# A one-row gate sum moved from TensorE matmuls to VectorE multiply-adds, in a four-layer conditional residual block

## The reference

```python
x = x + L0(x, lang)      # adapter 256 -> 64 -> 256 and a layer norm
x = x + L1(x, subj)      # one 256x256 matrix, chosen by subject
x = x + L2(x, type)      # five two-layer networks and a gate
x = x + L3(x, type)      # masked softmax pooling over the 512 rows

def L2(h, type_idx, ...):
    s0, s1, s2 = (relu(h @ share_wi[n]) @ share_wo[n] for n in range(3))      # 256 -> 1024 -> 256
    expert_out = out_a * wa + out_b * wb                                      # two experts, mixed
    gi = concatenate([expert_out[:, 0], s0[:, 0], s1[:, 0], s2[:, 0]])        # row 0 only, 4*256 numbers
    g = softmax(relu(gi @ gate_w1) @ gate_w2)                                 # gate_w1 is 1024x256, gate_w2 256x4
    return expert_out * g[0] + s0 * g[1] + s1 * g[2] + s2 * g[3]
```

## Time and profile before

| | |
|---|---|
| median of 3 runs | 563.62 us (563.46 to 563.65) |
| the profiled execution's own time | 563.65 us |
| its span, first to last instruction | 561.4 us |
| TensorE busy | 546.3 us, 97% of the span |
| VectorE, ScalarE, GpSimd busy | 316.3 us (56%), 262.7 us (47%), 257.8 us (46%) |
| mean granted clock of TensorE | 0.99 |
| chain that ended last | PE 91%, DVE 4%, the rest 1% or less each |

### The profile page before, as it was taken

The page is one execution under the profiler, slowest core; times in us unless marked ns, Lnnn a source line. Parts: engine busy times, 40 slices in busy tenths (PEclk is TensorE's granted clock), DMA queues, the critical chain, the costliest instruction groups (busy, mean ns, idle before and its releaser), DMA issues.

```text
span 561.4 us, 7437 instructions
## 1 busy us (share of the span) xinstructions
PE 546.3 (97%) x2724; PEld 452.3 (81%) x2727; DVE 316.3 (56%) x528; ACT 262.7 (47%) x481; POOL 257.8 (46%) x209
## 2 busy tenths in 40 slices
PE   5999999999999999999999999999999999999995
PEld 3578888888888788788888788888888878889984
DVE  3877323684366395566237478457326649522377
ACT  3345544443456562535246555334335647443343
POOL 1475355445244373444434447334524537744044
PEclk9899999999999999999899999999989999999999
DMA  5424424222224325024203422322222222420002
GB/s 155 142 100 145 122 76 150 76 75 76 75 76 123 93 77 165 27 73 129 83 20 118 144 97 76 112 76 76 75 75 77 76 75 88 138 76 0 2 1 76
DMA packets 44460, 49.34 MB, mean 88 GB/s; under 512 B 7300, under 2 KB 34184, under 8 KB 44424
## 3 DMA queue, kind: packets, MB, share of 16 engines
q1 hardware_dynamic: 43624, 47.81, 26.4%
q10 hardware_dynamic: 800, 1.05, 0.6%
HBM read 46.76 MB, written 2.10 MB: 87 GB/s over the span
## 4 chain that ended last, share of the span: by engine, by line
PE 91%; DVE 4%; POOL 1%; SPq 1%; issue 1%; DMA 1%; ACT 1%; DVEq 0%; POOLq 0%; ACTq 0%
PE ps_hid L707 13%; PE ps_hid L712 13%; PE ps_net L762 13%; PE ps_hid L708 13%; PE ps_net L763 13%; PE ps_net L767 12%; PE ps_side L561 2%; PE ps_side L424 1%; PE ps_side L429 1%; PE ps_side L425 1%; PE ps_net L736 1%; DMA beta<-in_L_cond_beta_dram 1%; PE ps_hid L546 1%; PE ps_side L625 1%; PE ps_side L631 1%
## 5 line engine op out<-in xcount | busy, mean ns | idle before, releaser
L1432 DVE SCALAR_TENSOR_TENSOR hid_lo<-ps_hid,hid_hi 128x512 fp32r<-128x512 f32 x160 | 110.2, 689 | 194.3 <-ACT hid_hi L937 194.0
L1514 POOL TENSOR_TENSOR wi_lo<-raw_wi,wi_hi 128x512 fp32r<-128x512 f32 x80 | 108.0, 1350 | 242.9 <-ACT wo_hi L918 142.6
L937 ACT ACTIVATE hid_hi<-ps_hid 128x512 fp32r<-128x512 f32 x160 | 95.5, 598 | 224.3 <-PE ps_hid L712 224.1
L707 PE MATMUL ps_hid<-x2T_hi,wi_lo 128*128 128x512 f32 (+1 forms) x338 | 127.8, 380 | 0.2 <-POOL wo_lo L1515 0.2
L708 PE MATMUL ps_hid<-x2T_hi,wi_hi 128*128 128x512 f32 (+1 forms) x338 | 127.0, 378 | 0.0
L762 PE MATMUL ps_net<-hid_hi,wo_hi 128*128 128x512 f32 x304 | 122.9, 404 | 0.0
L763 PE MATMUL ps_net<-hid_hi,wo_lo 128*128 128x512 f32 x304 | 120.0, 395 | 0.0
L1515 POOL TENSOR_TENSOR wo_lo<-raw_wo,wo_hi 128x512 fp32r<-128x512 f32 x80 | 106.5, 1331 | 0.0
L712 PE MATMUL ps_hid<-x2T_lo,wi_hi 128*128 128x512 f32 (+1 forms) x338 | 100.4, 378 | 1.1 <-DVE x2T_lo L1389 1.1
L767 PE MATMUL ps_net<-hid_lo,wo_hi 128*128 128x512 f32 x304 | 94.7, 393 | 0.0
L707 PEld LDWEIGHTS ps_hid<-x2T_hi,wi_lo 128*128 128x128 f32 x338 | 63.5, 188 | 12.5 <-POOL wo_lo L1515 0.4
(11 more groups left out here) (269 smaller groups left out, 608.4 us busy)
## 6 DMA issues: line engine op xcount, KB each, us to landing
raw_wi<-in_L_cond_share_wi_dram SPq DMA_DIRECT2D x23, 512.0 KB, 3.7
raw_wo<-in_L_cond_share_wo_dram SPq DMA_DIRECT2D x23, 512.0 KB, 4.7
raw_wi<-in_L_cond_expert_wi_dram SPq DMA_DIRECT2D x16, 512.0 KB, 3.6
raw_wo<-in_L_cond_expert_wo_dram SPq DMA_DIRECT2D x16, 512.0 KB, 4.6
x_rows<-in_x_dram SPq DMA_DIRECT2D x3, 512.0 KB, 6.1
out_dram<-out_rows SPq DMA_DIRECT2D x6, 256.0 KB, 2.4
subj_w<-in_L_cond_weight_dram SPq DMA_DIRECT2D x4, 256.0 KB, 2.5
gate_w<-in_L_cond_gate_w_dram SPq DMA_DIRECT2D x1, 1024.0 KB, 5.7
```

The costliest lines, as they stand in the source:

```text
L707: mm(dst, wi_lo[:, w, k, c], x2T_hi[:, k, rows], start=(k == 0), stop=False)
L937: fn(hid_hi[:, ring(b, q)], ps_hid[:, ring(b, q)], ACT.Relu).then_inc(hid_hi_ready, 1)
L1432: v.scalar_tensor_tensor(out=hid_lo[:, ring(b, q)], in0=ps_hid[:, ring(b, q)], scalar=0.0, in1=f32(hid_hi[:, ring(b, q)]), op0=ALU.max, op ...
L1514: g.tensor_tensor(wi_lo[:, w], raw_wi[:, half % 2, :, c], f32(wi_hi[:, w]), ALU.subtract)
```

## The change

The sum over weight rows goes to VectorE. A new tile `gate_acc` (128 partitions by 256) gathers, for each partition p, the weight rows p of all eight chunks, each multiplied by that partition's number of the output column: one instruction per chunk of 128 weight rows, eight per batch, each on 128x256. What is left is the sum over the 128 partitions, which TensorE makes with two matmuls of `gate_acc` against a column of ones. In the last batch the first three networks go through `gate_acc`, and the last one's four matmuls stay. The old `gate_sum` tile is renamed `gate_den`, and `gate_sum` is now the semaphore.

```diff
-    GATE_PART = SLOTS - 1
+    GATE_SUM = {20: 0, 27: 1, 38: 2}
...
-            def gate_terms(first_net, end_net):
-                if first_net == 0:
-                    pe.wait_ge(gate_in, 32)
-                for o in range(KD):
-                    for c in range(first_net * KD, end_net * KD):
-                        rows = GATE_OF[c // KD] * KD + c % KD
-                        last = mm(ps_side[:, 0, o:o + 1], gate_w1[:, rows, o * P:(o + 1) * P], netT[:, c // KD, c % KD, 0:1],
-                                  start=(o == 0 and c == 0), stop=(c == NG * KD - 1), skip_group_check=True)
+            def gate_columns(with_last):
+                for o in range(KD):
+                    cols, dst = slice(o * P, (o + 1) * P), ps_side[:, 0, o:o + 1]
+                    last = mm(dst, gate_acc[:, cols], ones[:, 0:1], start=(o == 0), stop=not with_last, skip_group_check=True)
+                    if with_last:
+                        for k in range(KD):
+                            last = mm(dst, gate_w1[:, GATE_OF[NG - 1] * KD + k, cols], netT[:, NG - 1, k, 0:1],
+                                      start=False, stop=(k == KD - 1), skip_group_check=True)
...
                 if slot == C_SLOT["gate"]:
-                    nets_in_sbuf(i, NG)
-                    gate_terms(NG - 1, NG).then_inc(c_pe.sem, 1)
+                    pe.wait_ge(a_dve.sem, a_dve.at(i + 1, "x2T0"))
+                    pe.wait_ge(gate_sum.sem, gate_sum.at(i, "g3k1"))
+                    gate_columns(False).then_inc(c_pe.sem, 1)
...
                 if slot == END_GATE:
+                    pe.wait_ge(gate_in, 32)
+                    pe.wait_ge(gate_sum.sem, gate_sum.at(B - 1, "g2k1"))
                     pe.wait_ge(e_act.sem, e_act.at(0, "last0"))
-                    gate_terms(NG - 1, NG).then_inc(e_pe.sem, 1)
+                    gate_columns(True).then_inc(e_pe.sem, 1)
...
-                    if last and 0 <= q - END_GATE_PART < NG - 1:
-                        nets_in_sbuf(b, q - END_GATE_PART + 1)
-                        gate_terms(q - END_GATE_PART, q - END_GATE_PART + 1)
-                    if not last and q == GATE_PART:
-                        pe.wait_ge(a_dve.sem, a_dve.at(b + 1, "x2T0"))
-                        nets_in_sbuf(b, NG - 1)
-                        gate_terms(0, NG - 1)
...
+            def add_gate_terms(i, net):
+                if net == 0:
+                    dve.wait_ge(gate_in, 32)
+                for k in (0, 1):
+                    by = evac_act if k == 1 else evac_dve
+                    dve.wait_ge(by.sem, by.at(i, f"g{net}"))
+                    weight, row = gate_w1[:, GATE_OF[net] * KD + k], netT[:, net, k, 0:1]
+                    if net == 0 and k == 0:
+                        v.tensor_scalar(gate_acc[:], weight, row, None, ALU.mult).then_inc(gate_sum.sem, 1)
+                    else:
+                        dve.wait_ge(gate_sum.sem, gate_sum.at(i, f"g{net}k{k}") - 1)
+                        v.scalar_tensor_tensor(out=gate_acc[:], in0=weight, scalar=row, in1=gate_acc[:],
+                                               op0=ALU.mult, op1=ALU.add).then_inc(gate_sum.sem, 1)
...
+                    if q in GATE_SUM and not (last and q == SLOTS - 2):
+                        add_gate_terms(b, GATE_SUM[q])
+                    if last and q == SLOTS - CH + 2:
+                        add_gate_terms(b, NG - 2)
                     if last:
                         last_gates(q)
                 if not last:
                     split_x2(b + 1)
                     evacuate(b, NG - 1)
+                    add_gate_terms(b, NG - 1)
```

More of the change, by code:

```diff
@@ L80, in cond_resid_program @@
     HALF0_END = SLOTS - CH // 2 - 1
-    END_BASE, END_GATE_PART, END_GATE = SLOTS // 2 + 2, SLOTS - CH + 1, HALF0_END + 2
+    END_BASE, END_GATE = SLOTS // 2 + 2, HALF0_END + 2
     WARM_XT, WARM_HID, WARM_ADAPT, WARM_SUBJ, WARM_NORM, WARM_HALF, WARM_X2, WARM_OUT = 8, 2, 3, 9, 6, 12, 3, 6
@@ L171, in cond_resid_program @@
         x3T = sb("x3T", [P, KD, S])
+        gate_acc = sb("gate_acc", [P, D])
         gate_h = sb("gate_h", [P, KD, P])
@@ L174, in cond_resid_program @@
         gate_e = sb("gate_e", [P, NG])
-        gate_sum = sb("gate_sum", [P, 1])
+        gate_den = sb("gate_den", [P, 1])
         gate_rec = sb("gate_rec", [P, 1])
@@ L231, in cond_resid_program @@
         p_pool = Steps(sem("p_pool"), "w1_lo w2_lo rstd0 rstd1 subj_w_lo")
+        gate_sum = Steps(sem("gate_added"), "g0k0 g0k1 g1k0 g1k1 g2k0 g2k1 g3k0 g3k1")
         c_pe = Steps(sem("c_pe"), "gate_h logits rows0 rows1 att score_row score_col out0 out1 out2 out3")
@@ L546, in keep_warm @@
                     mm(bank, zeros[:, 0:P], zeros[:], start=True, stop=True)
-            def nets_in_sbuf(i, nets):
-                pe.wait_ge(evac_act.sem, evac_act.at(i, f"g{nets - 1}"))
-                pe.wait_ge(evac_dve.sem, evac_dve.at(i, f"g{nets - 1}"))
-            def gate_terms(first_net, end_net):
-                if first_net == 0:
-                    pe.wait_ge(gate_in, 32)
-                for o in range(KD):
-                    for c in range(first_net * KD, end_net * KD):
-                        rows = GATE_OF[c // KD] * KD + c % KD
-                        last = mm(ps_side[:, 0, o:o + 1], gate_w1[:, rows, o * P:(o + 1) * P], netT[:, c // KD, c % KD, 0:1],
-                                  start=(o == 0 and c == 0), stop=(c == NG * KD - 1), skip_group_check=True)
+            def gate_columns(with_last):
+                for o in range(KD):
+                    cols, dst = slice(o * P, (o + 1) * P), ps_side[:, 0, o:o + 1]
[4 more added lines that the diff above has]
+                                      start=False, stop=(k == KD - 1), skip_group_check=True)
                 return last
@@ L833, in stage_c @@
                     act.wait_ge(c_dve.sem, c_dve.at(i, "gate_max"))
-                    fn(gate_e[:], ps_side[:, 1, 0:NG], ACT.Exp, bias=neg_gmax[:], accum_out=gate_sum[:]).then_inc(c_act.sem, 1)
+                    fn(gate_e[:], ps_side[:, 1, 0:NG], ACT.Exp, bias=neg_gmax[:], accum_out=gate_den[:]).then_inc(c_act.sem, 1)
                 if slot == C_SLOT["x3_split"]:
@@ L882, in last_gates @@
                     act.wait_ge(e_dve.sem, e_dve.at(0, "gate_max"))
-                    fn(gate_e[:], ps_side[:, 1, 0:NG], ACT.Exp, bias=neg_gmax[:], accum_out=gate_sum[:]).then_inc(e_act.sem, 1)
+                    fn(gate_e[:], ps_side[:, 1, 0:NG], ACT.Exp, bias=neg_gmax[:], accum_out=gate_den[:]).then_inc(e_act.sem, 1)
                 if slot == END_GATE + 1:
@@ L1086, in gate_chain @@
                     dve.wait_ge(act_s.sem, act_s.at(n, "gate_exp"))
-                    v.reciprocal(gate_rec[:], gate_sum[:]).then_inc(dve_s.sem, 1)
+                    v.reciprocal(gate_rec[:], gate_den[:]).then_inc(dve_s.sem, 1)
                     dve.wait_ge(dve_s.sem, dve_s.at(n, "gate_rec"))
```

## The result

The changed kernel takes 548.11 us (median of 4 runs, 548.04 to 548.93) where the one before took 563.54 (4 runs, 562.51 to 563.65): ratio 0.9723, 95% interval 0.9704 to 0.9742. The profiled execution took 548.15 us, its span is 546.4, so 1.75 us lie outside the span (2.25 before).

A forecast was written before the change was run, and what follows sets the result against it. TensorE's own instruction stream was taken as the bound from about 30 to 530 us. Savings of 11.31 + 1.32 + 1.34 = 13.97 us off 563.65 gave 549.7 us, with a range of 548.6 to 553.0 for 8 in 10.

The forecast's parts named there:

- Batch ends: Ends of batches 0 to 2: removing TensorE's block of twelve one-column gate matmuls saves 2.69 + 4.32 + 4.30 = 11.31 us.
- The clock: Behind the blocks of batches 1 and 2, TensorE's clock falls to half; without the blocks this loss goes, 3.2 us.
- The first rival: Clock falls at 277 and 410 us belong to the boundary or return elsewhere: up to 3.2 us back, 552.9 us; chance 0.16.
- Its milder form: Only one of the two clock falls returns, giving 551.3 us; part of the case with chance 0.16.
- The point made for the rival: The block ending batch 0 had no clock fall behind it, so the block alone doesn't decide; no size given.
- Slot 1: Slot 1 of batches 1 to 3: four gate matmuls become two on TensorE, saving 0.44 × 3 = 1.32 us.
- Last batch: Slots 33 to 35 lose gate matmul groups, slot 37 grows from four to six: 0.90 + 0.89 − 0.45 = 1.34 us saved.
- VectorE's links hidden: VectorE's 30 added 128x256 instructions, the links, at 0.5 us each, delay nothing at batch ends or in slots 20, 27, 34, 38.
- That only slot 38 would meet GpSimd: Of the places of VectorE's links, only slot 38 overlaps GpSimd; even at the bound 0.5 us is left.
- the rival that saw no gain: TensorE waits in slot 1 for late links, 4.7 us at each of three boundaries: 563.6 us or slower; chance 0.02.
- The step that failed: Closing step of the sum: profiled 563.65 us and the three-run median 563.62 taken as agreeing bases, within 0.03 us.

The follow-up runs named there:

- e4: The changed kernel with twelve unused one-column matmuls put back at the ends of batches 0 to 2, where the block stood: 559.64 us, ratio 0.9923.
- e14: The kernel before, with gamma and beta on a semaphore of their own so that VectorE's first cast no longer waits for beta: 561.92 us, ratio 0.9959.
- e8: The changed kernel with the last batch's four groups of four gate matmuls back and no VectorE terms in that batch: 550.65 us, ratio 0.9783.
- e3: The changed kernel without VectorE's 30 instructions of the gate's sum, the tile holding a constant: 550.85 us, ratio 0.9767.
- e15: The changed kernel with gamma and beta on a semaphore of their own: 546.25 us, ratio 0.9696.
- e5: The changed kernel with the twelve unused one-column matmuls put back as two groups of six, in slots 38 and 39: 556.76 us, ratio 0.9893.

## Why the prediction was right, and where it missed

- **Batch ends, 11.31 us.** Right. Putting the block back costs 2.66 + 4.29 + 4.31 = 11.26 us (e4).
- **The clock, 3.2 us of it.** Right in every profiled execution: none of the changed kernel shows a fall in the loop, and e4 brings both falls back. The Trainium skill ("TensorE: Matmul & The Clock Gate", what is actually happening) has activity release the throttle, and the trace agrees with the prediction's use of it, by which the loss belongs to the weakly loaded stretch: windows at 0.50 and 0.55 behind the block, 1.00 with the block halved. The first rival, as it stood (both falls back at the boundaries), is refuted. Its milder form, one fall that comes back elsewhere, is not: 4 of the 13 runs of the changed kernel have the longer span and the lower clock of one more fall, and none of them was profiled. They lie outside the first comparison, whose four runs all had 0.996 or 0.997. The point made for the rival, that the first block had no fall behind it, did not hold as an argument: in e14 the same block, 2.9 us sooner, had one. That fits what the same page of the Trainium skill (the two states) says of a freely running observation; no run moves the phase alone, so that is argued.
- **Slot 1, 1.32 us.** Right: what the segments give beyond e4's block prices is (3.08 − 2.66) + (4.79 − 4.29) + (4.74 − 4.31) = 1.35.
- **Last batch, 1.34 us.** Right (1.35 by segment; 1.27 in e8). The wait for `wo_lo` was forecast as one of 1.1 us and came as two, 0.19 and 0.61 by their rows, and 0.35 and 0.78 by starts.
- **VectorE's links hidden.** Right (e3). They were given 0.5 us each; the median is 485 ns, the mean 656, since those beside GpSimd take up to 1586. Slot 38's pair took 2.04 us, between the forecast and its bound, and nothing waited for it. That only slot 38 would meet GpSimd was wrong: in batch 0 slot 20's second link took 1.59 us beside it, free of charge as well. The sentence of the Trainium skill on the shared read interface ("SBUF — State Buffer", who interferes with whom) agrees with these two places in size: the link took 1.1 us more than its median, beside GpSimd instructions of 1.29 us. In the rival that saw no gain the links would have had to take (290.4 − 284.0)/2 = 3.2 us each, not 2.6, which makes it less likely still.
- **The step that failed** is the last of the sum: "The median of the three runs is 563.62, so the two bases agree within 0.03 us." The profiled execution's start and its 2.25 us outside the span were carried over to the changed kernel as if they were fixed, which puts two terms at nothing. The first, 1.12 us, has to do with no part of the change: the start is one of two about 1.1 us apart, set by the landing of `beta` (e14, e15), and in the comparison the changed kernel mostly had the early one and the kernel before the late one. That is chance. The second, 0.50 us, goes with the program: every run of the changed kernel has 1.74 to 1.83 us outside the span, and every run of the kernel before 2.06 to 2.26. This is part of what the change gave; its cause stays open. With both the same sum gives 563.65 − 1.12 − 0.50 − 13.97 = 548.06 us, where 548.11 was measured. With the first alone it would be 548.56, with the second alone 549.18. On the second chip the same kernel took 550.48 us, so the measured median owes its place to the mix of levels in four runs. The range looked for its uncertainty in the change alone and had none for the base.

## What to carry to other kernels

One-column matmuls in plain float32 are dear on a TensorE that bounds the kernel: here about 0.11 us a record, where a matmul of 256 columns in rounded parts took 0.12, and an unbroken run of 24 records can cost the clock for the next 3 us as well. Split such a run if it can't be moved (e5), and give the sum to an engine that has idle time. When you forecast a median from one profiled execution, ask which of its stretches hang on a DMA's landing, and widen the range by what these vary; compare by segments between fixed instructions, not by spans alone.

## What the runs showed of the hardware that was not expected

- The start varies in steps: the cast that waits for `beta`, a transfer of 1 KB with two numbers to a partition, began at 10.50 to 10.82 us in seven profiled executions and at 11.47 to 11.98 in eight, and the whole program moved with it.
- The granted clock fell behind a run of 24 one-column records in the three batch ends of e14, in two of three in e4 and in the kernel before, and behind none of the runs of 12 records in e5, all in profiled executions; the loss was 1.6 us each time.
- A level about 1.5 us longer, with a mean granted clock 0.003 lower, comes in some runs of both kernels, with the block and without it; no profiled execution caught it.
- The time outside the span has two levels, about 1.8 and 2.1 to 2.2 us, that go with the program and not with the run; no experiment found what sets them.
- Four independent VectorE instructions on 128x256 took 1.67 us, a dependent pair 1.07 us.
